# The decay exponents of a state-space layer: from TensorE products to rows read back from memory, GpSimd and ScalarE

## The chip, the cores and the metric

One core of one Trainium2 chip runs the whole program. The time is device microseconds of that core. TensorE (PE) multiplies and transposes, VectorE (DVE), ScalarE (ACT) and GpSimd (POOL) do the rest, and SyncE's queue (SP) starts nearly all transfers. The kernel before takes 5693.69 us, the median of 3 runs (5674.86 to 5695.94).

## The reference

Two transformer-like layers over 64 batches of 128 tokens with 256 channels, all in float32. Layer 0 is a state-space layer (Mamba-2 form), a cross attention and a mixture of 16 experts; layer 1 is an attention, a cross attention and a quantized product. Only the first matters here:

```python
dt = jax.nn.softplus(dt_in + dt_bias)          # 32 heads
A_bar = jnp.exp(-jnp.exp(A_log) * dt)
def step(h, inp):
    ab, dtt, bt, ct, xt = inp
    h = ab[..., None, None] * h + (dtt[..., None] * bt)[:, :, None, :] * xt[..., None]
    return h, jnp.einsum('bhn,bhpn->bhp', ct, h)
```

The kernel writes the recurrence as a product. With cum(t) the running sum of |A| dt up to token t, head h of token t gets the sum over s <= t of (C_t . B_s) exp(-(cum(t) - cum(s))) dt_s x_s. For each head this is a 128 x 128 matrix of exponents, 32 of them for a batch.

## The kernel before, in words

The program has three phases. The first takes each batch through four chains: M (norm, input projection, convolution, softplus), N (the exponents, the products of the heads, gate, output projection), X (cross attention of layer 0) and F (router, shared expert). They are pipelined over the batches: an iteration of the loop does M of batch n, N of n-1, X of n-2 and F of n-3. The second phase runs the experts, the third layer 1 in the same manner. The change touches only the first.

Each engine has its own instruction list, and the table ORDER (line 48) fixes by hand in which order it takes the steps of the four chains: `Nv3` is step v3 of chain N, `Mip1` step ip1 of chain M. Engines meet through semaphores: `tell` raises one, `done` waits for this batch's, `was` for the previous batch's. An engine never goes past a step that waits. `link` makes an engine wait for its own last result.

The way of the exponents before:

- DVE step Msp (lines 712 to 727): 18 small dependent operations on 128 x 32 tiles make softplus by a series, ending in `a`, the decay times dt, spread over the rows of `aGL`.
- PE step MGL: two products with the triangle `triu` make the running sums; ACT copies them to `GL`; POOL step MR (line 547) makes from them `R`, 128 x 1024, with a mask that picks a head in each row.
- PE steps Na0 to Na7 (line 1383): each multiplies 19 rows of GL by 19 rows of R, and so writes the differences of the running sums of four heads into a PSUM bank, 128 x 512.
- ACT Ne0 to Ne7 (line 1123) takes the exponential, DVE Nm0 to Nm7 (line 768) takes the minimum with 1 and multiplies with `cbm`, the masked C.B product, and PE Nv0 to Nv7 (line 1398) multiplies with x dt.

```python
tell(mm(Q[4 if k in (1, 3) else 2][:, :], GL[rows, 1, :], R[rows, 4 * u:4 * u + 4, :], start=True, stop=True), "arg")
tell(s_.activation(Edw[k % 2], Q[4 if k in (1, 3) else 2][:, :], ACT.Exp), "E")
tell(v.scalar_tensor_tensor(Mh[k % 2], Ed[k % 2], 1.0, cbm.unsqueeze(1).broadcast_to([P, 4, T]), ALU.min, ALU.mult), "M")
```

After the heads: ACT copies both banks (Yt), PE transposes them (Ny0, Ny1), DVE adds the skip term to `y2` (line 773) and multiplies with the gate `gz` (Nyg, line 778), ACT sums its squares (Nsq), POOL makes the root mean square (Nrms, lines 553 and 554), PE transposes (NyT) and projects (Npr), and DVE makes `x1` (Nx1, line 785). In the next iteration X norms x1: DVE statistics (Xln2, line 671), POOL (lines 539 and 540), DVE (Xln2n, line 675), PE transposition (Xln2n).

X scores its 16 heads in four strips of the key rows (line 1318, Xs0 to Xs3), each after a mask product (line 1417), in banks Q5, Q6, Q5, Q6. DVE takes row maxima (line 682), ACT exponentials (lines 1082 and 1085), PE transposes them (line 1324, Xt0 to Xt3), and DVE (line 693) and ACT (line 1092) evacuate two of the four each.

Of the kernel before, what the change touches and what calls it, by code (L numbers as in the profile page):

```python
# [13 lines left out]
F32 = mybir.dt.float32  # L14
# [6 lines left out]
ALU = mybir.AluOpType  # L21
# [3 lines left out]
P = 128  # L25
# [64 lines left out]
def two_layers(nc, x_d, ctx_d, m0_d, m1_d, w_in, conv_w, conv_b, a_log, d_p, dt_bias, norm_w, w_out,  # L90
# [5 lines left out]
    slot_d = nc.dram_tensor("slot_rows", (NB, T, 4), U32)  # L96
    with ExitStack() as ctx:
# [65 lines left out]
        Apos = sb("Apos", [P, NH])  # L163
# [11 lines left out]
        aGL = sb("aGL", [P, 2, P])  # L175
        pick = sb("pick", [P, 8])
# [8 lines left out]
        base = sb("base", [P, NE])  # L185
        table = sb("table", [1, 3, TILES], I32)
# [20 lines left out]
        cbm, GL, R = part(T), cut(part(2 * T), 2), part(8 * T).rearrange("p (h t) -> p h t", t=T)  # L207
        Edw, Mhw = [part(512), part(512)], [part(512), part(512)]
        Ed = [e.rearrange("p (h t) -> p h t", t=T) for e in Edw]
        Mh = [e.rearrange("p (h t) -> p h t", t=T) for e in Mhw]  # L210
        Yt = part(2 * DI)
        sq0, yT, yg, y2 = Edw[0], cut(Edw[1], IC), Mhw[0], Mhw[1]
# [52 lines left out]
        spread = lambda k: aGL[:, k, :].rearrange("p (i r) -> p i r", i=4)[:, :, 8 * k:8 * k + 8].rearrange("p i (u j) -> p u i j", u=2)  # L265

        for n in ("xa_in", "xr_in", "ctx0_in", "mask0_in", "meta_out", "xo_out", "meta_in", "x2s_in", "ctx1_in", "mask1_in", "out_done"):
            sig(n, 16)
        sig("scattered", 32)  # L270
        sig("gathered", 32)
        signals("M", "DVE", "ln1_var ln1_xn dt_pre a conv cbm xs2 gz xdt")
        signals("M", "PE", "ln1_Tps ip2 ip1 z CB GLps xsT")
        signals("M", "ACT", "ln1_T dt_abs bcT dt_exp xpad tz conv_th GL")
        signals("M", "POOL", "ln1_rstd R")
        signals("N", "DVE", "M:8 y2 yg x1")
        for n, k in (("arg", 8), ("Yk", 8), ("Yb", 2), ("yTps", 1), ("mamba", 1), ("E", 8), ("Yt", 2), ("ss", 1), ("yT", 1), ("rms", 1)):
            sig(n, k)
        signals("X", "DVE", "ln2_var ln2_xn mrow k0c S0max:4 PT0v:2 x2")
        signals("X", "PE", "ctxTps ln2_Tps k0 qv0 S0:4 PT0ps:4 PV0:2")  # L280
        signals("X", "ACT", "ctxT ln2_T q0c v0c P0:4 PT0s:2 OT0")
# [23 lines left out]
        links = {"M_DVE": 18, "X_DVE": 5, "F_DVE": 15, "A_DVE": 5, "K_DVE": 3, "L_DVE": 11, "M_POOL": 1, "N_POOL": 1, "X_POOL": 1,  # L305
# [65 lines left out]
        def _(sp):  # L371
# [126 lines left out]
        def _(pool):  # L498
# [1203 lines left out]
```

## Time and profile before

| | |
|---|---|
| median of 3 runs | 5693.69 us |
| the profiled execution's own time | 5707.57 us |
| its span | 5705.7 us |
| PE busy | 5197.1 us (91%) |
| DVE busy | 3886.4 us (68%) |
| ACT busy | 2510.9 us (44%) |
| POOL busy | 1489.5 us (26%) |
| mean granted TensorE clock | 0.876 |
| first phase | to about 2860 us |
| costliest line of the first phase | L1383, 684.7 us |

The profile of one execution lists for every engine what it was busy with, what it waited for, and which transfer or engine released it. Busy times of an engine can't be compared with the span alone: what counts is which of the waits ends last in the stage in question.
### The profile page before, as it was taken

The page shows a single profiled execution, that of the slowest core. Times are in us where ns is not written, and L with a number is a line of the kernel's source. Part 1 is how long each engine was busy: PE and PEld are TensorE (multiplying, and loading weights), DVE is VectorE, ACT ScalarE, POOL GpSimd, SP SyncE. Part 2 cuts the span into 40 slices and gives each one's busy share as a digit, 9 for nine tenths or more (in the row PEclk, how much of TensorE's full clock was granted, in tenths as well). Part 3 has the DMA queues.
Part 4 walks back from the last instruction along what each step waited for, and adds up shares of the span by engine and source line. Part 5 has one row for each costly group of instructions (what it writes and reads, how often), then busy time and mean ns, then how long its engine had stood idle before and what let it go on. Part 6 is the DMA issues. An engine that isn't in the chain of part 4 may idle for free.

```text
span 5705.7 us, 117447 instructions
## 1 busy us (share of the span) xinstructions
PE 5197.1 (91%) x33556; PEld 3331.3 (58%) x33683; DVE 3886.4 (68%) x10535; ACT 2510.9 (44%) x6582; POOL 1489.5 (26%) x2225
## 2 busy tenths in 40 slices
PE   5999999999999999999957779999999999999997
PEld 3656656656655665665535546666666666666564
DVE  3767776777776777776633337777777777777776
ACT  1444443444444444443322235555555555555554
POOL 1211121121121122112100014444444444344343
PEclk8878887888887888887767779999999999999999
DMA  3000000000000000000022210000000000000000
GB/s 103 19 17 17 17 22 17 18 20 17 17 22 17 17 20 18 17 17 22 16 74 88 88 45 19 18 18 18 18 18 18 18 18 18 18 18 18 14 18 13
DMA packets 153161, 146.76 MB, mean 26 GB/s; under 512 B 39392, under 2 KB 142112, under 8 KB 153120
## 3 DMA queue, kind: packets, MB, share of 16 engines
q1 hardware_dynamic: 134208, 102.98, 6.1%
q0 software_dynamic: 12288, 33.57, 1.9%
q10 hardware_dynamic: 6624, 9.70, 0.5%
q8 instruction: 21, 0.34, 0.0%
q14 instruction: 20, 0.16, 0.0%
HBM read 91.38 MB, written 54.79 MB: 26 GB/s over the span
## 4 chain that ended last, share of the span: by engine, by line
PE 49%; issue 20%; DVE 11%; POOL 9%; DMA 5%; ACT 3%; SPq 2%; POOLq 0%; DVEq 0%; ACTq 0%
PE Q L1288 11%; PE Q L1383 11%; PE Q L1295 6%; PE Q L1318 5%; PE Q L1300 4%; PE Q L1490 4%; PE Q L1398 4%; DMA arena<-in_ctx_dram 2%; POOL mvK L540 2%; POOL l L596 2%; DMA meta<-slot_rows 2%; DVE arena L739 2%; DVE arena L693 1%; PE Q L1502 1%; PE Q L1417 1%
## 5 line engine op out<-in xcount | busy, mean ns | idle before, releaser
L1300 PE MATMUL Q<-ident,arena 128*128 128x128 f32 x4768 | 847.5, 298 | 237.7 <-DVE arena L962 75.5
L1300 PEld LDWEIGHTS Q<-ident,arena 128*128 128x128 f32 x4768 | 589.6, 152 | 614.6 <-issue 244.7
L1383 PE MATMUL Q<-arena 19*128 19x512 f32 x1024 | 684.7, 828 | 47.3 <-ACT arena L1123 43.5
L1123 ACT ACTIVATE arena<-Q 128x512 f32<-128x512 f32 x512 | 300.0, 599 | 564.7 <-PE Q L1383 563.2
L1295 PE MATMUL Q<-Wkvl,arena 128*128 128x512 f32 x1024 | 513.2, 625 | 1.6 <-ACT arena L1074 0.9
L553 POOL TENSOR_TENSOR ss<-ss,eps 128x1 f32<-128x1 f32 x64 | 12.2, 191 | 1918.2 <-ACT arena L1133 1918.2
L596 POOL TENSOR_TENSOR l<-l,half_pow 128x8 f32<-128x8 f32 x192 | 330.0, 1719 | 583.5 <-DVE l L958 583.5
L682 DVE TENSOR_REDUCE mx<-Q 128x4 f32<-128x512 f32 x512 | 351.0, 686 | 54.6 <-PE Q L1318 33.1
L768 DVE SCALAR_TENSOR_TENSOR arena<-arena 128x512 f32<-128x512 f32 x512 | 348.8, 687 | 50.0 <-ACT arena L1123 49.1
L1318 PE MATMUL Q<-arena 32*128 32x128 f32 x4096 | 374.0, 284 | 9.1
L1318 PEld LDWEIGHTS Q<-arena 32*128 32x128 f32 x4096 | 312.6, 187 | 116.5 <-issue 116.5
L1324 PEld LDWEIGHTS Q<-ident,arena 128*128 128x128 f32 x2048 | 245.3, 142 | 111.1 <-issue 68.5
L1262 ACT ACTIVATE arena<-Q,mxl 128x256 f32<-128x256 f32 x512 | 236.6, 474 | 158.4 <-DVE mxl L994 158.4
L1085 ACT ACTIVATE arena<-Q,mx 128x128 f32<-128x128 f32 x1024 | 291.1, 375 | 1.4 <-DVE mx L682 1.4
L1324 PE MATMUL Q<-ident,arena 128*128 128x128 f32 x2048 | 289.1, 274 | 1.2 <-ACT arena L1082 0.5
L1383 PEld LDWEIGHTS Q<-arena 19*128 19x128 f32 x1024 | 168.6, 227 | 203.0 <-issue 103.0
L1295 PEld LDWEIGHTS Q<-Wkvl,arena 128*128 128x128 f32 x1024 | 186.6, 201 | 170.6 <-issue 155.0
L1490 PE MATMUL Q<-Wgu,arena 128*128 x576 | 212.2, 503 | 72.4 <-issue 54.6
L1071 ACT ACTIVATE arena<-Q 128x256 f32<-128x256 f32 x256 | 98.3, 384 | 388.3 <-PE Q L1300 388.3
L1288 PE MATMUL Q<-arena,Win 128*128 128x128 f32 x1536 | 252.3, 314 | 0.0
L1288 PEld LDWEIGHTS Q<-arena,Win 128*128 128x128 f32 x1536 | 215.7, 217 | 62.0 <-issue 62.0
L1398 PE MATMUL Q<-arena 128*16 128x128 f32 x4096 | 243.5, 330 | 0.0
(292 smaller groups left out, 10672.7 us busy)
## 6 DMA issues: line engine op xcount, KB each, us to landing
arena<-routed_rows SPq DMA_DIRECT2D x144, 128.0 KB, 2.0
expert_rows<-arena SPq DMA_DIRECT2D x144, 128.0 KB, 1.7
arena<-in_x_dram SPq DMA_DIRECT2D x128, 128.0 KB, 2.1
arena<-in_ctx_dram SPq DMA_DIRECT2D x128, 128.0 KB, 2.2
x_rows<-arena SPq DMA_DIRECT2D x64, 128.0 KB
arena<-x_rows SPq DMA_DIRECT2D x64, 128.0 KB, 2.0
out_dram<-arena SPq DMA_DIRECT2D x64, 128.0 KB, 1.7
routed_rows<-arena SPq DMA_DIRECT2D x17, 128.0 KB, 1.7
```

The lines of the kernel that those rows point to most:

```text
L596: link(pool, "K_POOL", b, g.tensor_tensor(l2[:, k, :], l2[:, k, :], half_pow[:, :], ALU.pow), bare=True)
L682: largest = v.tensor_reduce(mx[:, 4 * j:4 * j + 4], pj, AX.X, ALU.max, negate=True)
L768: tell(v.scalar_tensor_tensor(Mh[k % 2], Ed[k % 2], 1.0, cbm.unsqueeze(1).broadcast_to([P, 4, T]), ALU.min, ALU.mult), "M")
L1123: tell(s_.activation(Edw[k % 2], Q[4 if k in (1, 3) else 2][:, :], ACT.Exp), "E")
L1288: last = mm(out, lhs(c), rhs(c), start=c == 0, stop=c == n - 1)
L1295: last = mm(out, lhs(c), rhs(c), start=c == 0, stop=c == n - 1)
L1300: last = nc.tensor.transpose(out[:, c * P:(c + 1) * P], src[:, c * P:(c + 1) * P], ident[:, :])
L1318: last = mm(banks[j][:, g * T:(g + 1) * T], QT[r, g, :], KT[r, g // 2, :], start=False, stop=g == NG - 1)
L1324: last = nc.tensor.transpose(bank[:, g * T:(g + 1) * T], S[:, j, g, :], ident[:, :])
L1383: tell(mm(Q[4 if k in (1, 3) else 2][:, :], GL[rows, 1, :], R[rows, 4 * u:4 * u + 4, :], start=True, stop=True), "arg")
L1398: last = mm(Q[3 + k // 4][32 * i:32 * i + HP, (k % 4) * T:(k % 4 + 1) * T], xdt[:, h * HP:(h + 1) * HP], Mh[k % 2][:, i, :], start=True, s ...
L1490: last = mm(Q[2 + s % 2][:, 0:2 * FF], xeT[s % 4][:, c, :], Wgu[:, bass.ds(e, 1), c, :].rearrange("p a f -> p (a f)"), start=c == 0, stop= ...
```

## The change

The exponents no longer come from TensorE. The running sums go out to a table in memory (`cum_rows`), 32 x 128 floats for a batch, and come back in four loads, each of which gives all 128 partitions the same 1024 values (8 heads x 128 tokens) in one of four tiles `Ew`. POOL subtracts from each the partition's own sum (Nd0 to Nd3), ACT takes the absolute value and then exp(-x) in place (Ng, Ne), and the product with `cbm` follows in place, for three tiles on DVE (Nm0 to Nm2), for the fourth on POOL (Nm3). PE takes eight heads in one step (Nv0 to Nv3). The tiles `R`, `GL`, `aGL` and `pick` go, with what sets them up.

Further: the softplus series moves from DVE to POOL, in another form (terms in pairs, 13 operations behind `ratio`); the gate product Nyg moves from DVE to POOL; cross attention has a third PSUM bank, Q2, so that strips 0, 1 and 2 are scored in one step; and ACT makes all four of its evacuations. ORDER is rewritten for all five queues.

```diff
@@ ORDER[1]
         "SP": """
-            Xc Nx Mx Fm Fo
+            Ncb0 Xc Ncb1 Ncb2 Ncb3 Nx Mx Fm Mco Fo
         "POOL": """
-            Xx1r Fln3 Xln2 Mln1 Nrms Fsc MR
+            Xx1r Xln2 Fln3 Nd0 Mln1 Nd1 Nd2 Nd3 Nm3 Msp Fsc Nyg Nrms
...
@@ SP
+                yield "co"
+                done(sp, "cumT", b)
+                tell(sp.dma_start(rows(cum_d, b), cumT[0:NH, :]), "cum_out", 16)
...
+                for j in range(4):
+                    yield f"cb{j}"
+                    if j == 0:
+                        done(sp, "cum_out", b, 16)
+                    was(sp, "Yk", b, j + 1)
+                    heads8 = cum_d[bass.ds(b, 1), 8 * j:8 * j + 8, :].rearrange("a h t -> (a h t)")
+                    tell(sp.dma_start(Ew[j], heads8.partition_broadcast(P)), f"wide{j}", 16)
@@ POOL
+                yield "sp"
+                J = lambda ins: link(pool, "M_POOL", b, ins, bare=True)
+                s, z, z2, z4 = dts[:, 2, :], dts[:, 3, :], dts[:, 4, :], dts[:, 5, :]
+                done(pool, "ratio", b)
+                J(g.tensor_tensor(z, s, s, ALU.mult))
+                tell(g.tensor_tensor(z2, z, z, ALU.mult), "square")
+                J(g.tensor_tensor(terms, coef[:, 0, :, :], z.unsqueeze(1).broadcast_to([P, 4, NH]), ALU.mult))
...
+                J(g.tensor_tensor(dts[:, 6, :], terms[:, 0, :], dts[:, 0, :], ALU.add))
+                tell(g.tensor_tensor(dts[:, 7, :], dts[:, 6, :], Aneg[:, :], ALU.mult), "a")
...
+                    yield f"d{j}"
+                    if j == 0:
+                        done(pool, "cums", b)
+                    done(pool, f"wide{j}", b, 16)
+                    tell(g.tensor_tensor(E8[j], E8[j], cums[:, 8 * j:8 * j + 8].unsqueeze(2).broadcast_to([P, 8, T]), ALU.subtract), "diff")
+                yield "m3"
+                done(pool, "E", b, 4)
+                done(pool, "cbm", b)
+                tell(g.tensor_tensor(E8[3], E8[3], cbm.unsqueeze(1).broadcast_to([P, 8, T]), ALU.mult), "M3")
+                yield "yg"
+                done(pool, "y2", b)
+                tell(g.tensor_tensor(yg, gz, y2, ALU.mult), "yg")
@@ DVE
                 J(v.tensor_scalar(dts[:, 5, :], u, 2.0, None, ALU.add))
                 J(v.reciprocal(dts[:, 5, :], dts[:, 5, :]))
-                J(v.tensor_tensor(s, u, dts[:, 5, :], ALU.mult))
...
+                tell(v.tensor_tensor(dts[:, 2, :], u, dts[:, 5, :], ALU.mult), "ratio")
...
-                for k in range(8):
-                    yield f"m{k}"
...
+                for j in range(3):
+                    yield f"m{j}"
+                    done(dve, "E", b, j + 1)
+                    tell(v.tensor_tensor(E8[j], E8[j], cbm.unsqueeze(1).broadcast_to([P, 8, T]), ALU.mult), "M")
@@ ACT
+                tell(s_.activation(cums, Q[0][:, 2 * T:2 * T + NH], ACT.Copy), "cums")
+                tell(s_.activation(cumT[0:NH, :], Q[0][0:NH, 3 * T:4 * T], ACT.Copy), "cumT")
...
+                for j in range(4):
+                    yield f"g{j}"
+                    done(act, "diff", b, j + 1)
+                    tell(s_.activation(Ew[j], Ew[j], ACT.Abs), "gap")
+                    yield f"e{j}"
+                    done(act, "gap", b, j + 1)
+                    tell(s_.activation(Ew[j], Ew[j], ACT.Exp, scale=-1.0), "E")
@@ PE
-                for k in range(2):
-                    last = mm(Q[0][:, (2 + k) * T:(3 + k) * T], aGL[:, k, :], triu[:, :], start=True, stop=True)
...
+                mm(Q[0][:, 2 * T:2 * T + NH], triu[:, :], dts[:, 7, :], start=True, stop=True)
+                tell(mm(Q[0][0:NH, 3 * T:4 * T], dts[:, 7, :], triu[:, :], start=True, stop=True), "cumps")
...
-                strips(b, banks, (0, 1), QT0, KT0, 0, mask)
-                for j in (2, 3):
-                    yield f"s{j}"
-                    done(pe, "S0max", b, j - 1)
-                    strips(b, banks, (j,), QT0, KT0, 0, mask)
+                strips(b, banks, (0, 1, 2), QT0, KT0, 0, mask)
+                yield "s3"
+                done(pe, "S0max", b)
+                strips(b, banks, (3,), QT0, KT0, 0, mask)
```

TensorE at the head of the loop's body, before: line 1300 transposes the context, line 1383 are the exponent products, line 1398 the heads, and the third row of line 1300 is the transposition of the normed x1.

```order
L1300 MATMUL Q<-ident,arena 128x128 x2
L1383 MATMUL Q<-arena 128x512 x2
L1383 MATMUL Q<-arena 128x512
L1398 MATMUL Q<-arena 16x128 x4
L1383 MATMUL Q<-arena 128x512
L1398 MATMUL Q<-arena 16x128 x4
L1300 MATMUL Q<-ident,arena 128x128 x2
L1383 MATMUL Q<-arena 128x512
L1288 MATMUL Q<-Wr,arena 128x16 x2
L1300 MATMUL Q<-ident,arena 128x128 x2
```

And now (the lines are those of the changed file; 1311 transposes, 1299 multiplies, 1395 are the heads):

```order
L1311 MATMUL Q<-ident,arena 128x128 x2
L1311 MATMUL Q<-ident,arena 128x128 x2
L1299 MATMUL Q<-arena,Wk 128x128 x4
L1311 MATMUL Q<-ident,arena 128x128 x2
L1299 MATMUL Q<-arena,Wq 128x128 x4
L1299 MATMUL Q<-Wr,arena 128x16 x2
L1311 MATMUL Q<-ident,arena 128x128 x2
L1299 MATMUL Q<-Wv,arena 128x256 x2
L1299 MATMUL Q<-Win,arena 128x32 x2
L1299 MATMUL Q<-arena,Win 128x128 x4
L1395 MATMUL Q<-arena 16x128 x8
```

The transposition of the normed x1 has moved from behind the fourth exponent product and two heads' steps to the second place, and the first heads' step stands behind the input projection's first piece.

GpSimd in one body of the loop now, from the last subtractions to the root mean square (576 are the subtractions, 580 the product m3, 552 to 568 the series, 604 the scatters of F, 583 the gate product):

```order
L576 TENSOR_TENSOR arena<-arena 128x1024 x3
L580 TENSOR_TENSOR arena<-arena 128x1024
L552 TENSOR_TENSOR arena<-arena 128x32
L553 TENSOR_TENSOR arena<-arena 128x32
L554 TENSOR_TENSOR arena<-coef,arena 128x128
...
L568 TENSOR_TENSOR arena<-arena,Aneg 128x32
L604 DMA routed_rows<-arena,meta 133248x256 x2
L583 TENSOR_TENSOR arena<-arena 128x512
L586 TENSOR_TENSOR ss<-ss,eps 128x1
L587 TENSOR_TENSOR ss<-ss,half_pow 128x1
```

Before, this queue had only the small steps of the norms, the scatters and one 1024-wide product in a body; series and gate product were VectorE's. Now both scatters stand between the series and the gate product.

## Rows read from the trace of the kernel before

**Rows 1.** Windows of the whole program: length, busy of PE, PEld, DVE, ACT, POOL, granted clock, DMA

```profile
1000.00:2300.00 1300.00, 1258.34 (x8313) 784.48 (x8312) 938.28 (x2873) 553.49 (x1394) 257.54 (x360) 0.82 0.06 18
...
2850.00:2950.00 100.00, 52.42 (x203) 34.26 (x203) 35.64 (x91) 17.16 (x55) 2.76 (x4) 0.62 0.22 67
```

**Rows 2.** Line 547, one instruction in an iteration: number, duration, first and last start

```profile
L547 POOL TENSOR_TENSOR arena<-arena,pick x64: 1895/1908/2132, 70.7 to 2792.0; 128x1024 f32<-128x1024 f32 x64
```

**Rows 3.** Windows of single iterations of the first phase, same columns, last the sum and mean of 16

```profile
1400.73:1441.44 40.71, 39.29 (x276) 24.88 (x275) 30.94 (x96) 18.27 (x46) 8.73 (x13) 0.87 0.06 19
1441.44:1488.24 46.80, 45.38 (x275) 27.90 (x274) 30.86 (x95) 18.27 (x46) 8.72 (x12) 0.74 0.05 17
...
sum 685.94, PE 663.50 PEld 414.46 DVE 495.65 ACT 292.29 POOL 137.02; mean PE 41.47 PEld 25.90 DVE 30.98 ACT 18.27 POOL 8.56
```

**Rows 4.** Windows of 2 us, PE busy, granted clock, DMA share and GB/s

```profile
1542.00:1544.00 2.00, 2.00 (x3) 0.50 0.00 0
...
1574.00:1576.00 2.00, 2.00 (x12) 1.00 0.69 223
```

**Rows 5.** Groups by line, window 1000 to 2300, the operations that go

```profile
L1383 PE MATMUL Q<-arena 19*128 19x512 f32 x482 | 319.0, 818 | 20.4 <-ACT arena L1123 20.4
...
L768 DVE SCALAR_TENSOR_TENSOR arena<-arena 128x512 f32<-128x512 f32 x243 | 165.3, 687 | 16.0 <-ACT arena L1123 15.7
L1123 ACT ACTIVATE arena<-Q 128x512 f32<-128x512 f32 x242 | 141.9, 599 | 261.6 <-PE Q L1383 261.6
...
L547 POOL TENSOR_TENSOR arena<-arena,pick 128x1024 f32<-128x1024 f32 x30 | 57.3, 1909 | 0.6
...
L693 DVE COPY arena<-Q 128x512 f32<-128x512 f32 x60 | 40.9, 682 | 0.0
...
L721 DVE SCALAR_TENSOR_TENSOR arena<-arena 128x32 f32<-128x32 f32 x180 | 34.5, 192 | 6.1
```

**Rows 6.** Timeline of PE, window 1536 to 1579

```profile
1538.24 1.12 PE L1383 MATMUL Q<-arena 19*128 19x512 f32 x2 [0.68 <-ACT arena L1123]
...
1560.78 1.15 PE L1318 MATMUL Q<-arena 32*128 32x128 f32 x8
```

**Rows 7.** Timeline of PE in the third phase

```profile
4432.16 1.17 PE L1318 MATMUL Q<-arena 32*128 32x128 f32 x24
```

**Rows 8.** Groups by line, window 1000 to 2300, rows that bound the new operations

```profile
L571 POOL DMA_INDIRECT routed_rows<-arena,meta x60 | 60.8, 1014 | 17.6 <-issue 17.6
...
L1082 ACT ACTIVATE arena<-arena 128x512 f32<-128x512 f32 x62 | 35.3, 620 | 0.0
...
L560 POOL TENSOR_TENSOR arena<-arena,bv0b 128x256 f32<-128x256 f32 x30 | 21.7, 724 | 37.4 <-DVE arena L805 37.4
...
L539 POOL TENSOR_TENSOR mvX<-mvX,eps 128x1 f32<-128x1 f32 x30 | 17.7, 588 | 12.9 <-DVE mvX L672 12.8
...
L553 POOL TENSOR_TENSOR ss<-ss,eps 128x1 f32<-128x1 f32 x30 | 5.7, 191 | 895.5 <-ACT arena L1133 895.5
```

**Rows 9.** Timeline of all engines, window 1539 to 1541.5

```profile
1538.83 0.42 DVE L671 BATCH_NORM_STATS2 stX<-arena 128x6 f32<-128x256 f32 x1
...
1539.51 0.69 DVE L768 SCALAR_TENSOR_TENSOR arena<-arena 128x512 f32<-128x512 f32 x1
...
1539.66 0.59 POOL L539 TENSOR_TENSOR mvX<-mvX,eps 128x1 f32<-128x1 f32 x1 [0.99 <-DVE mvX L672]
...
1540.97 0.41 DVE L675 TENSOR_SCALAR arena<-arena,mvX 128x256 f32<-128x256 f32 x1 [0.44 <-POOL mvX L540]
```

**Rows 10.** Windows of DVE alone, from the convolution of one iteration to its end

```profile
1562.50:1577.02 14.52, 12.53 (x34) 1.00 0.11 36
```

**Rows 11.** Windows of 2 us in the third phase, same columns

```profile
4412.00:4414.00 2.00, 0.48 (x3) 1.00 0.23 67
...
4416.00:4418.00 2.00, 2.00 (x4) 0.50 0.23 66
...
4420.00:4422.00 2.00, 2.00 (x12) 1.00 0.00 0
```

More of the change, by code:

```diff
@@ L206, in two_layers @@
         bcT, dts = cut(part(2 * T), 2), cut(part(8 * NH), 8)
[L207 to L210, printed above, removed]
+        terms = cut(part(4 * NH), 4)
+        cbm, cumT, cums = part(T), part(T), part(NH)
+        Ew = [part(8 * T) for _ in range(4)]
+        E8 = [e.rearrange("p (h t) -> p h t", t=T) for e in Ew]
         Yt = part(2 * DI)
-        sq0, yT, yg, y2 = Edw[0], cut(Edw[1], IC), Mhw[0], Mhw[1]
+        sq0, yT = Yt[:, 0:DI], cut(Yt[:, DI:2 * DI], IC)
+        yg, y2 = part(DI), part(DI)
         xr, x1, x1r, x2, o0 = part(D), part(D), part(D), part(D), part(D)
@@ L512, in _ @@
             g.memset(triu[:], 1.0)
-            g.memset(aGL[:], 0.0)
-            g.memset(pick[:], 0.0)
             g.memset(before[:], 1.0)
+            for k in range(8):
+                g.memset(coef[:, 1 - k % 2, k // 2, :], 2.0 / (2 * k + 1))
             g.memset(ones[:], 1.0).then_inc(SEM["pads"], 1)
@@ L525, in _ @@
                             pattern=[[1, P]], channel_multiplier=-1)
-            picked = [(32 * i + 8 * k, -1) for i in range(4) for k in range(2)] + [(32 * i + 16 + c, 0) for i in range(4) for c in range(3)]
-            for n, (row, step) in enumerate(picked):
-                g.affine_select(out=pick[:, :], in_=pick[:, :], compare_op=ALU.not_equal, fill=1.0, base=-row,
-                                pattern=[[step, 8]], channel_multiplier=1).then_inc(SEM["pads"], 1)
-                pool.wait_ge(SEM["pads"], n + 2)
             g.affine_select(out=causal[:, :, :], in_=causal[:, :, :], compare_op=ALU.is_ge, fill=NEG, base=0,
@@ L631, in _ @@
             dve.wait_ge(SEM["consts"], 1)
-            rows = aGL[:, :, :].rearrange("p k (i r) -> p k i r", i=4)
-            for k in range(2):
-                v.memset(rows[0:1, k, :, 8 - 8 * k:16 - 8 * k], 1.0)
-            for c in range(3):
-                here, after = slice(32 * c, 32 * c + 1), slice(32 * c + 32, 32 * c + 33)
-                v.memset(rows[here, 0, :, 16 + c:17 + c], 1.0)
-                v.memset(rows[after, 0, :, 16 + c:17 + c], -1.0)
-                v.memset(rows[after, 1, :, 16 + c:17 + c], BLOCKED)
             for bank in (Q[3], Q[4]):
@@ L745, in M @@
                 done(dve, "CB", b)
-                was(dve, "M", b, 8)
+                was(dve, "M3", b)
                 tell(v.tensor_tensor(cbm, Q[0][:, 0:T], triu[:, :], ALU.mult), "cbm")
@@ L756, in M @@
                 done(dve, "xsT", b)
-                was(dve, "Yk", b, 8)
+                done(dve, "a", b)
+                was(dve, "Yk", b, 4)
                 was(dve, "y2", b)
@@ L787, in X @@
             def X(b):
-                banks = (Q[5], Q[6], Q[5], Q[6])
+                banks = (Q[6], Q[2], Q[5], Q[6])
                 yield "ln2"
@@ L1086, in softmax, with evac @@
                     tell(last, f"P{n}")
-            def evac(b, banks, PT, n):
-                for j in (1, 3):
+            def evac(b, banks, PT, n, js=(1, 3)):
+                for j in js:
                     yield f"t{j}"
@@ L1154, in X @@
                 yield from softmax(b, banks, S0, mx0, 0)
-                yield from evac(b, banks, PT0, 0)
+                yield from evac(b, (Q[2], Q[5], Q[6], Q[2]), PT0, 0, range(4))
                 yield "OT"
@@ L1339, in M @@
                 yield "ln1n"
-                was(pe, "GL", b)
+                was(pe, "cumT", b)
                 lnT("ln1", xn0, Q[0], b)
@@ L1413, in X @@
             def X(b):
-                banks = (Q[5], Q[6], Q[5], Q[6])
+                banks = (Q[6], Q[2], Q[5], Q[6])
                 def mask(bank):
```

164 lines of the change are left out of this document (65 added, 99 removed).

## The prediction

> **What bounds the kernel now.** I read the windows first. In the steady part of the first phase TensorE is busy 97% of the time, VectorE 72%, ScalarE 43% and GpSimd 20% [rows 1]. One R product of GpSimd comes in each iteration, 64 of them from 70.7 to 2792.0 us, so an iteration takes 2721.3/63 = 43.2 us [rows 2]. TensorE works 41.5 us of it [rows 3]. The kernel's first half is bound by TensorE, and 1 us less in an iteration is worth 64 us. The third phase and the expert phase are not touched.
>
> The clock belongs to this reading. Iterations take 40.7 us at a granted clock of 0.87 and 46.8 us at 0.74 [rows 3]. The clock is at one of two levels, 1.2 or 2.4 GHz, so the low time is 2 x (1 - 0.87) x 40.7 = 10.6 us in the one and 24.3 us in the other. 6.1 us more for 13.7 us of low time: a low microsecond costs 0.44 us. The mean clock of 0.82 [rows 1] means 15.6 us of low time, 6.9 us an iteration. It falls soon after the iteration's head, where two short waits and the 19-row exponent products lie, and stays low with TensorE fully busy [rows 4].
>
> **TensorE.** The eight exponent products go: 319.0 us in 1300 us, 10.5 us an iteration [rows 5]. At the full clock one is 1.12 us [rows 6]. Cross attention's scores of strips 0, 1 and 2 are now one step over three banks. Before, strip 2 was a step of its own, 1.15 us [rows 6]; in the third phase, which has this form, three strips take 1.17 us together [rows 7]. That is 1.1 us less. The two cumulative products get smaller, 0.3 us. So 41.5 - 10.5 - 1.1 - 0.3 = 29.6 us of work stay, at the present mix of clocks.
>
> **The other engines**, in an iteration. VectorE loses eight 512-wide products (5.45 us), 13 of the 32-wide steps (2.5 us), two 512-wide evacuations (1.36 us) [rows 5] and one 512-wide gate product (0.7 us). It gains three 1024-wide ones; 512 take 0.687 us and 32 take 0.192, so 1024 take 1.21 us, 3.6 us. 31.0 becomes 24.6 us. ScalarE: eight 512-wide exponentials (4.8 us) go, eight 1024-wide passes come. A 512-wide one between SBUF tiles is 0.620 us [rows 8]; twice is 1.24, and with some 0.2 us of start-up counted once it is 1.04, 8.3 us in all. With two evacuations of 0.6 us more, 18.3 becomes 23.1 us. GpSimd: the one 1.91 us product becomes five of that size (9.5 us), a 512-wide one (between 0.72 us for 256 and 1.91 us for 1024: 1.1 us) and 13 small dependent steps. Nothing shows such a step on GpSimd. Its bounds are 0.19 us (one element) and 0.72 us (256 elements) [rows 8], plus 0.07 us to the next: 3.4 to 10.3 us for 13. Most have 32 elements, two have 128; I take 0.42 us each, 5.5 us. 8.6 becomes about 22 us. So no engine's work alone reaches TensorE's 29.6 us. What the order makes them wait for decides.
>
> **The new chain.** The iteration ends with x1, and its first dense step is the transposition of the normed x1, second in TensorE's new order. Before, three exponent products and more stood ahead of it. From the statistics to the normed rows took 2.55 us, 1538.83 to 1541.38 [rows 9]. The statistics can start 0.7 us after TensorE's last product, and the 0.4 us transposition of the context covers little. TensorE is idle for about 3 us at each head, against 43.2 - 41.5 = 1.7 us in a whole iteration before.
>
> The second piece is longer. The softplus series starts from `ratio`, which VectorE now makes after the last row maximum of cross attention. In the window from the convolution to the iteration's end VectorE is busy 12.5 us [rows 10]; less a maximum, the two evacuations and the gate product, and with the last sum, 10.2 us stay behind `ratio`. So 24.6 - 10.2 = 14.4 us of work stand ahead of it, and waits: for both norms' GpSimd answers, the second of them behind the first 1.91 us subtraction, for the first exponential (1.9 + 2 x 1.04 us after its data), for the rank product, for the scores. I estimate 7.6 us, and `ratio` at 22 us after x1. Then, in GpSimd's order, the series (5.5), the two scatters (1.01 each and 0.3 between [rows 8], 2.6 us) and the gate product (1.1), then on TensorE the transpositions NyT, MxsT and XOT and the projection (about 0.9, 0.9, 0.9, 1.9 us), then x1 (0.7 with its wait), and 0.2 us of handovers. 22 + 5.5 + 2.6 + 1.1 + 4.6 + 0.7 + 0.2 = 36.7 us. This is over TensorE's 29.6 + 3 = 32.6 us, so my forecast is that TensorE waits, mainly ahead of NyT: **36.7 us an iteration**. 43.2 - 36.7 = 6.5 us, times 64 is 416 us. The profiled execution's own time is 5707.6 us, 14 us above the median of the runs shown; 5707.6 - 416 = 5292, rounded **5290 us**.
>
> **SP and DMA.** An iteration adds 16 KB out and four loads of 512 KB. A window with a DMA share of 0.69 moved 223 GB/s [rows 4], so 2 MB need 6.5 us at the full 323 GB/s. The first waits for the sums, about 5 us before x1; the context load stands behind it, the x load behind all four. I place x at 3.0 us after x1, just when VectorE wants it: hidden, with no slack. The set-up loses 0.6 us of VectorE's and about 6 us of GpSimd's selections; those lie under the weight loads.
>
> **A rule against the change.** VectorE's 512-wide product of two SBUF tiles ran from 1539.51 to 1540.20; GpSimd's one-element sum, started at 1539.66, took 0.59 us [rows 9], against 0.191 us for the same sum elsewhere [rows 8]. It ended when the product did. So the two block each other. The Trainium skill (SBUF — State Buffer, Who interferes with whom) says the same: an instruction of VectorE with two SBUF inputs and one of GpSimd that reads SBUF exclude each other for the whole instruction. The trace agrees. I have 1.5 us of such waits in the 7.6.
>
> For the long subtractions I took the 1.91 us of the R product [rows 2], the same engine, width and kind. The Trainium skill (GPSIMD Engine Reference, Elementwise — side-by-side cycle accounting) gives 4497 ns for a sum of 2048 elements; an estimate from that page is 2.25 us for 1024, by which the five would take 1.7 us more and the iteration would be up to 38.4 us. The row decides.
>
> **Rivals.**
> **1. TensorE stays the bound.** If `ratio` and the series come earlier than I estimate, the head alone counts: 29.6 + 3.2 = 32.8 us, 10.4 x 64 = 666 us, 5040 us. For it: my 7.6 us are a guess. Against it: gate product and scatters stand in line behind the series.
> **2. The loads are late.** At half the rate the 2 MB take 6.5 us longer; x, last in line, arrives some 4.5 us late, and VectorE's list slips with it: 41.2 us, 5580 us. Against it: the window's 223 GB/s.
> **3. The two engines lock.** The three 1024-wide VectorE products each wait for most of a 1.91 us subtraction, and half the series' steps take the 0.59 us of [rows 8] or more: some 3.5 + 1 us, again 41 us, 5580 us. Against it: before the change one iteration shows only a few such meetings, but it has only one long GpSimd product.
> **4. The clock stays low: slower.** The 29.6 us hold about 3.7 us of low-clock cost that remains (6.9 less the removed products' own share of 3.2: 10.5 us as they ran, 7.3 at the full clock, where one pair runs side by side and another beside the scores): 25.9 us at the full clock. If TensorE, waiting more often, is granted 2.4 GHz for a fraction 1 - f of the time, the iteration is 25.9 + 3 + 0.44 f P. It passes the old 43.2 at f = 0.75 (clock 0.62). At f = 0.8 it is 44.6 us, plus 90 us, 5798 us; at f = 1, 51.6 us. For it: a stretch with TensorE busy 52% has a clock of 0.62 [rows 1]. Against it: in the third phase an idle head of 1.5 us in 2 costs one low stretch, and dense products bring the clock back within 6 us [rows 11]; behind the new head come dense 128-row products, not the 19-row ones.
>
> **Chances and range.** Forecast 0.46 (its own range 35 to 39 us: 5180 to 5440), rival 1 0.22, rival 2 0.09, rival 3 0.10, rival 4 0.09, no change 0.04 (gains and waits just cancel). A measurement of this kernel tells 0.5% (28 us) from nothing. Faster: 0.46 + 0.22 + 0.09 + 0.10 = 0.87; same 0.04; slower 0.09. From 5000 to 5600 us only rival 4, the null case and the edges are left out, 2 in 10; the bounds of the series (2.1 us less or 4.8 more, times 64: 5155 to 5600) lie inside.
>
> **What the new profile should show.** No 19-row products; PE busy near 30 us in an iteration of 36 to 38; idle TensorE at the head for the normed x1 (3 us) and ahead of NyT for GpSimd's product (over 1 us); `ratio` at 22 us; series steps of 0.3 to 0.5 us; the 1024-wide subtraction near 1.9 us; a clock of 0.8 to 0.9. Wrong would be: the wide loads as the releaser of GpSimd or of the first statistics (rival 2), subtractions or steps far over these sizes (rival 3), a clock under 0.65 (rival 4), or a period under 34 us (rival 1).

## The result and the profile after

The changed kernel takes 5699.2 us (median of 20 runs, 5691.2 to 5713.7) and the kernel before 5683.6 us (20 runs). The ratio is 1.0028, with a 95% interval of 1.0018 to 1.0037: no difference worth the name, where 5290 us had been forecast. The profiled execution has a span of 5694.8 us. The windows after, with the columns of [rows 1] and [rows 3]; the second line is one iteration of the first phase, from the end of one x1 nearly to the end of the next:

```profile
1000.00:2300.00 1300.00, 980.45 (x7676) 736.59 (x7675) 968.40 (x2209) 681.62 (x1458) 679.93 (x896) 0.84 0.20 67
...
1578.57:1622.40 43.83, 31.99 (x258) 24.17 (x258) 32.10 (x75) 22.77 (x49) 22.78 (x30) 0.84 0.21 70
```

x1 comes 37 times from 926.6 to 2492.5 us, so an iteration takes 43.5 us, as against 43.2 before. What TensorE does has fallen, from 1258 to 980 us in this stretch, or 41.5 to 32.0 us an iteration (29.6 had been forecast), at nearly the same clock (0.82, then 0.84). All of it came back as idle time: TensorE now stands still for 12 us of 44. VectorE was to fall from 31.0 to 24.6 us and is still at 32.1. The waits of the same stretch (what waited for what: us in total, times, longest):

```profile
PE Q L1311 <- DVE arena L699: 145.5, 66, 5.3
DVE arena L768 <- POOL arena L583: 109.4, 30, 3.7
...
DVE stM L695 <- DMA arena<-in_x_dram: 74.0, 30, 3.6
...
PE Q L1311 <- POOL arena L583: 63.4, 30, 2.1
PE Q L1311 <- DMA arena<-in_ctx_dram: 54.6, 30, 3.2
PE Q L1376 <- POOL arena L568: 38.2, 30, 1.4
```

L699 is VectorE's normalization ahead of the transpositions, L583 GpSimd's gate product, L695 the statistics of the next batch's x, L568 the end of the softplus series. Three different things hold TensorE: slow norms, late loads, and the gate product. The next groups by line (shapes apart; busy, mean ns of one, idle before) say why the norms are slow:

```profile
L576 POOL TENSOR_TENSOR arena<-arena 128x1024 f32<-128x1024 f32 x120 | 255.8, 2152 | 0.0
L781 DVE TENSOR_TENSOR arena<-arena 128x1024 f32<-128x1024 f32 x90 | 148.1, 1645 | 0.0
L580 POOL TENSOR_TENSOR arena<-arena 128x1024 f32<-128x1024 f32 x30 | 87.4, 2913 | 240.9 <-ACT arena L1135 240.9
L699 DVE TENSOR_SCALAR arena<-arena,mvF 128x256 f32<-128x256 f32 x30 | 59.3, 1976 | 3.6
L699 DVE TENSOR_SCALAR arena<-arena,mvM 128x256 f32<-128x256 f32 x30 | 59.3, 1975 | 28.1 <-POOL mvM L543 28.1
L829 DVE TENSOR_SCALAR rt<-rt 128x16 f32<-128x16 f32 x30 | 50.3, 1677 | 1.1
L739 DVE TENSOR_SCALAR arena<-arena 128x32 f32<-128x32 f32 x29 | 33.3, 1148 | 0.0
...
L699 DVE TENSOR_SCALAR arena<-arena,mvX 128x256 f32<-128x256 f32 x30 | 12.4, 412 | 4.0
```

The same 256-wide normalization takes 412 ns for mvX and 1976 ns for mvF and mvM; a step of 16 columns takes 1677 ns. The timeline of an ordinary iteration (start, us, engine, line; VectorE, GpSimd and TensorE rows) shows what runs beside them:

```profile
1580.32 0.41 DVE L699 TENSOR_SCALAR arena<-arena,mvX 128x256 f32<-128x256 f32 x1
1580.58 0.66 PE L1311 MATMUL Q<-ident,arena 128*128 128x128 f32 x4 [3.17 <-DMA arena<-in_ctx_dram]
1581.11 1.89 POOL L576 TENSOR_TENSOR arena<-arena 128x1024 f32<-128x1024 f32 x1
1581.18 1.98 DVE L699 TENSOR_SCALAR arena<-arena,mvF 128x256 f32<-128x256 f32 x1
...
1586.22 0.43 DVE L695 BATCH_NORM_STATS2 stM<-arena 128x6 f32<-128x256 f32 x1 [3.07 <-DMA arena<-in_x_dram]
...
1587.85 6.63 POOL L576 TENSOR_TENSOR arena<-arena 128x1024 f32<-128x1024 f32 x3
1587.92 1.98 DVE L699 TENSOR_SCALAR arena<-arena,mvM 128x256 f32<-128x256 f32 x1 [0.94 <-POOL mvM L543]
1589.95 0.69 PE L1311 MATMUL Q<-ident,arena 128*128 128x128 f32 x2 [5.05 <-DVE arena L699]
1590.23 2.50 DVE L781 TENSOR_TENSOR arena<-arena 128x1024 f32<-128x1024 f32 x1
1592.83 1.68 DVE L829 TENSOR_SCALAR rt<-rt 128x16 f32<-128x16 f32 x1
...
1606.00 0.19 DVE L741 TENSOR_TENSOR arena<-arena 128x32 f32<-128x32 f32 x1
```

Each norm starts just after a subtraction (L576) and ends just after it: 1581.18 + 1.98 is 1583.16, the subtraction ended at 1583.00. It doesn't run slowly, it stands until GpSimd is done. That looks like the lock of [rows 9], on instructions that had not been counted. The three subtractions in a row (6.63 us, where three times 1.89 would be 5.67) hold the third norm, then the first product, then the router step, which ends at 1594.51, when the last of them has ended (1594.48). The 1.0 us beyond 5.67 is about what the last subtraction would have to wait for the end of the product (1592.73): VectorE seems to hold GpSimd in turn. The end of the same iteration:

```profile
1612.35 0.25 POOL L568 TENSOR_TENSOR arena<-arena,Aneg 128x32 f32<-128x32 f32 x1 [0.18 <-POOL arena L567]
...
1612.73 0.40 PE L1376 MATMUL Q<-arena,triu 128*128 128x32 f32 x2 [1.40 <-POOL arena L568]
...
1613.21 1.28 POOL L604 DMA_INDIRECT routed_rows<-arena,meta  x1 [0.61 <-issue]
...
1615.79 1.27 POOL L583 TENSOR_TENSOR arena<-arena 128x512 f32<-128x512 f32 x1
1617.11 2.82 PE L1311 MATMUL Q<-ident,arena 128*128 128x128 f32 x12 [2.11 <-POOL arena L583]
1617.17 0.69 DVE L768 SCALAR_TENSOR_TENSOR arena<-arena,Q 128x512 f32<-128x512 f32 x1 [3.65 <-POOL arena L583]
1617.78 0.42 DVE L855 TENSOR_TENSOR arena<-Q,arena 128x256 f32<-128x256 f32 x1
...
1622.28 0.48 DVE L795 SCALAR_TENSOR_TENSOR arena<-Q,ss,arena 128x256 f32<-128x256 f32 x1 [0.33 <-PE Q L1306]
```

GpSimd's gate product (L583) stands behind the series and two scatters. VectorE's gate for the next batch (L768) must not write `gz` before that product has read it, so VectorE waits 3.65 us. Behind it stands `xo` (L855), and for `xo` waits a store that is ahead of all loads in SP's queue. SP's own timeline, around the end of the iteration before:

```profile
1570.85 0.35 SPq L412 DMA_DIRECT2D cum_rows<-arena  x1
1575.03 0.34 SPq L439 DMA_DIRECT2D x_rows<-arena  x1
1576.08 0.35 SPq L421 DMA_DIRECT2D arena<-cum_rows  x1
1576.71 0.35 SPq L429 DMA_DIRECT2D arena<-in_ctx_dram  x1
1577.35 0.25 SPq L431 DMA_DIRECT2D mask0i<-in_mask_BxS_ik_dram  x1
1577.97 1.44 SPq L421 DMA_DIRECT2D arena<-cum_rows  x3
1579.66 0.33 SPq L424 DMA_DIRECT2D arena<-in_x_dram  x1
1580.27 0.33 SPq L409 DMA_DIRECT2D arena<-in_x_dram  x1
```

The first wide load goes out at 1576.08, 2.5 us before the end of x1 (1578.57); the two loads of x are last, behind 2 MB. From 1578 to 1584, in windows of 1 us, the share of the DMA engines is 0.92 to 1.10 and they move 239 to 384 GB/s: the loads are not slow, they are asked for late.

TensorE's clock, in windows of 2 us of the same iteration (length, PE busy, granted clock, DMA share, GB/s):

```profile
1586.00:1588.00 2.00, 0.00 (x0) 0.56 0.00 0
1590.00:1592.00 2.00, 2.00 (x6) 0.50 0.00 0
1598.00:1600.00 2.00, 2.00 (x27) 1.00 0.04 1
```

It falls to its lower level while TensorE stands still for 5.05 us, and stays there for some 7.5 us of dense products behind the wait. Around the wait of 2.11 us at the end it falls again (0.50 from 1618 to 1620); behind the 3.17 us at the head it was 1.00.

### The profile page after: what moved, and what is told of

Same layout as the page of the kernel before. It is cut to its first block, busy times and chain, and to the rows that moved or that the text cites. A ratio compares the mean times of both kernels' runs of the same rounds, so it can differ in the third digit from the quotient of the medians.

```text
span 5694.8 us, 115799 instructions
## 1 busy us (share of the span) xinstructions
PE 4605.1 (81%) x32658; PEld 3218.1 (57%) x32659; DVE 3970.2 (70%) x9179; ACT 2805.1 (49%) x6774; POOL 2398.2 (42%) x3363
## 4 chain that ended last, share of the span: by engine, by line
issue 32%; POOL 23%; PE 20%; DVE 14%; ACT 5%; DMA 2%; SPq 2%; POOLq 1%; DVEq 1%; ACTq 0%
PE Q L1306 7%; PE Q L1311 4%; PE Q L1486 4%; POOL arena L580 3%; POOL mvK L543 2%; POOL arena L576 2%; POOL l L629 2%; ACT arena L1132 2%; DMA meta<-slot_rows 2%; DVE rt L829 2%; PE Q L1299 2%; POOL arena L583 1%; POOL routed_rows L604 1%; PE Q L1329 1%; PE Q L1498 1%
## 5 line engine op out<-in xcount | busy, mean ns | idle before, releaser
L1311 PE MATMUL Q<-ident,arena 128*128 128x128 f32 x4768 | 861.1, 306 | 764.6 <-DVE arena L699 346.4
L576 POOL TENSOR_TENSOR arena<-arena 128x1024 f32<-128x1024 f32 x256 | 545.6, 2152 | 7.8 <-DMA arena<-cum_rows 7.8
L580 POOL TENSOR_TENSOR arena<-arena 128x1024 f32<-128x1024 f32 x64 | 186.1, 2908 | 510.7 <-ACT arena L1135 510.7
L781 DVE TENSOR_TENSOR arena<-arena 128x1024 f32<-128x1024 f32 x192 | 315.4, 1643 | 3.4 <-ACT arena L1135 3.4
L1329 PEld LDWEIGHTS Q<-arena 32*128 32x128 f32 x4096 | 251.4, 188 | 102.7 <-issue 102.7
L1335 PE MATMUL Q<-ident,arena 128*128 128x128 f32 x2048 | 307.0, 279 | 0.5 <-ACT arena L1091 0.5
L1329 PE MATMUL Q<-arena 32*128 32x128 f32 x4096 | 300.6, 285 | 0.0
L1132 ACT ACTIVATE arena<-arena 128x1024 f32<-128x1024 f32 x256 | 269.3, 1052 | 7.9 <-POOL arena L576 7.9
L1135 ACT ACTIVATE arena<-arena 128x1024 f32<-128x1024 f32 x256 | 269.5, 1053 | 6.1
L1299 PEld LDWEIGHTS Q<-arena,Win 128*128 128x128 f32 x1536 | 243.1, 237 | 46.8 <-issue 46.7
L1299 PE MATMUL Q<-arena,Win 128*128 128x128 f32 x1536 | 267.1, 329 | 0.0
L1101 ACT ACTIVATE arena<-Q 128x512 f32<-128x512 f32 x384 | 232.7, 614 | 54.2 <-PE Q L1335 54.2
```

The costliest lines, as they stand in the source:

```text
L576: tell(g.tensor_tensor(E8[j], E8[j], cums[:, 8 * j:8 * j + 8].unsqueeze(2).broadcast_to([P, 8, T]), ALU.subtract), "diff")
L580: tell(g.tensor_tensor(E8[3], E8[3], cbm.unsqueeze(1).broadcast_to([P, 8, T]), ALU.mult), "M3")
L781: tell(v.tensor_tensor(E8[j], E8[j], cbm.unsqueeze(1).broadcast_to([P, 8, T]), ALU.mult), "M")
L1132: tell(s_.activation(Ew[j], Ew[j], ACT.Abs), "gap")
L1299: last = mm(out, lhs(c), rhs(c), start=c == 0, stop=c == n - 1)
L1311: last = nc.tensor.transpose(out[:, c * P:(c + 1) * P], src[:, c * P:(c + 1) * P], ident[:, :])
```

## The experiments

Ratios are to the kernel before, timed beside each, with 95% intervals; the changed kernel's is 1.0028, and what a repair gives is counted from there, in times of 5684 us.

**The locks.** The subtraction on one column only:

```diff
-  tell(g.tensor_tensor(E8[j], E8[j], cums[:, 8 * j:8 * j + 8].unsqueeze(2).broadcast_to([P, 8, T]), ALU.subtract), "diff")
+  tell(g.tensor_tensor(Ew[j][:, 0:1], Ew[j][:, 0:1], cums[:, 8 * j:8 * j + 1], ALU.subtract), "diff")
```

> Leaves out the subtraction of the running sums but for one column of each wide tile, so the exponents are not the reference's; everything that waits for it still does. Theory L (the long GpSimd instructions block VectorE's: the norms of F and M, the first exponent product and the router's scaling took 1.98, 1.98, 2.50 and 1.68 us instead of 0.41, 0.41, 1.21 and 0.23, some 5.9 us in an iteration of 43.3): these go back to their short times, VectorE's ratio comes 4 to 5 us earlier after x1 (26 us now), the iteration falls to about 38.5 us, the total to about 5390. Theory D (the loads come too late: the x rows at 6.2 us after x1, the context at the head): the wait for the x rows only grows by what the norm of F gains, ratio comes at most 2.5 us earlier, total 5530 or more.

Measured: 5539.3 us, 0.9733 (0.9715 to 0.9751), in the range of Theory D and not at the 5390 of Theory L. The norms are back at 413 ns, the products at 1219, the router step at 234: the locks were real. But the wait for x grows from 74.0 us in 30 iterations to 146.9 in 32, because the statistics are now ready for it earlier:

```profile
DVE stM L695 <- DMA arena<-in_x_dram: 146.9, 32, 5.7
...
PE Q L1311 <- DVE arena L699: 119.1, 41, 5.4
DVE arena L768 <- POOL arena L583: 113.2, 31, 3.7
```

So the subtractions cost 168 us even while the load is late, and the load's wait takes up part of what they free. This is not the price of the locks alone, since GpSimd's queue has also become shorter.

**Which instructions lock.** The same, and fills of about the subtraction's length behind it, which read nothing:

```diff
+  g.memset(dump[:, j, :], 0.5)
+  tell(g.memset(Ew[j][:, 1:], 0.5), "diff")
```

> Leaves out the same subtraction, but GpSimd is kept as long as before at each of the four places, some 1.9 us, by two fills that read nothing. Told apart: if what counts is only that GpSimd's reads meet VectorE's second input, VectorE's norms and products run at their short times and the total is within 1% of that with one column. If fills block as well (every long GpSimd instruction locks), the norms of F and M (one SBUF input) stay near 2 us and the total near 5690. Theory D expects near 5690 too, but with short norms and a longer wait for the x rows.

Measured: 5651.4 us, 0.9923 (0.9906 to 0.9940), between the two totals named: 112 us above the run with one column, 60 under the changed kernel. Groups of VectorE by line:

```profile
L784 DVE TENSOR_TENSOR arena<-arena 128x1024 f32<-128x1024 f32 x90 | 109.5, 1217 | 0.0
...
L702 DVE TENSOR_SCALAR arena<-arena,mvF 128x256 f32<-128x256 f32 x31 | 55.5, 1789 | 3.7
L702 DVE TENSOR_SCALAR arena<-arena,mvM 128x256 f32<-128x256 f32 x31 | 55.3, 1784 | 28.9 <-POOL mvM L544 28.9
```

The product of two tiles runs free beside a fill (1217 ns, 1645 on average beside subtractions, which hold one in three); the norm, with one tile as input, is still held (1789 ns), and so is the router step (1518 ns). There are two kinds of lock, and the second needs no read on GpSimd's side. With the products free and the norms held, most of what the one-column run had gained is gone again.

**The loads.** SP issues the loads of x ahead of the wide ones:

```diff
-  Ncb0 Xc Ncb1 Ncb2 Ncb3 Nx Mx Fm Mco Fo
+  Xc Mx Ncb0 Ncb1 Ncb2 Ncb3 Nx Fm Mco Fo
```

> SP's order is Xc Mx Ncb0 Ncb1 Ncb2 Ncb3 Nx Fm Mco Fo: context and x rows are asked for ahead of the four wide loads. Theory D: VectorE's wait for the x rows (1.6 us at 1541 us, up to 3.6) and most of TensorE's wait for the context (54.6 us in 30 iterations, 1.8 each) go; 2 to 3.5 us an iteration, total 5470 to 5570. Theory L: M's statistics come earlier but its norm then waits for the GpSimd answer behind the next subtraction, or the wide loads come later; under 1 us an iteration, total 5640 or more.

Measured: 5546.6 us, 0.9737 (0.9720 to 0.9755), as Theory D had it. The wait for x is gone from the list. In the iteration of this kernel that begins with x1's end at 1530.96, the statistics of x start at 1535.47, 4.5 us later instead of 7.65 (1578.57 to 1586.22 above). The order also changes the locks: the first wide load comes later, and the norm of F takes 1158 ns on average instead of 1976, since some of them no longer meet a subtraction.

**The gate product**, back on VectorE behind y2:

```diff
@@ POOL
-  Msp Fsc Nyg Nrms
+  Msp Fsc Nrms
@@ DVE
-  Ny0 Ny1 Mxs2
+  Ny0 Ny1 Nyg Mxs2
```

> The gate product goes back from GpSimd to VectorE, right behind the skip sums; nothing else. Theory Q (the gate product stands behind series and scatters in GpSimd's queue; TensorE waits 2.1 us for it ahead of the projection, VectorE 3.65 us with the gate of the next batch, and behind that the residual, its store and the context load): both waits go, the iteration falls 2.5 to 4 us, total 5440 to 5540. Rival: VectorE is what bounds, and 0.7 us more of work costs 45 us: 5740.

Measured: 5535.3 us, 0.9723 (0.9707 to 0.9740), in the range of Theory Q. Both waits are gone. Left are TensorE's for the norms (143.7 us) and the loads: 95.7 us of TensorE's for the context and 106.9 us of VectorE's for x, in 32 iterations.

**The series**, back on VectorE in its old form, the rest as changed:

> The series from `ratio` to the decay steps goes back to VectorE in its old form; the rest stays as changed. On GpSimd it takes 6.3 us from `ratio`, on VectorE (from the 0.22 us between its instructions before) about 2.9. Theory P (the slow series is part of the bound, TensorE's 1.3 us ahead of the cumulated steps being its cost): 5694 - 64 x 1.3 = about 5610. Theory Q (what binds is the wait of the gate product's tail and the late loads; the convolution now starts 2.9 us later instead, and the cumulated steps wait for it): 5640 to 5740, no gain. I expect Q.

Measured: 5744.1 us, 1.0094 (1.0066 to 1.0121), slower than the changed kernel itself and 4 us above the range of Q. So moving GpSimd's 6.4 us series back gains nothing: VectorE has the work instead, and what follows on it comes later (VectorE busy 1013.83 of 1300 us, where it was 968.40).

**Both repairs**, loads and gate:

> The two correct repairs together: the loads of the residual and of the next input ahead of the wide loads, and the gate product back on VectorE. Alone they gave 0.9737 and 0.9723. If each removes a wait of its own (additive), the product is 0.947, about 5390. If both only free the same start of the next iteration (the late loads hide behind the gate's tail), they give little more than one alone: 5480 to 5540. I expect the first, 5370 to 5430, with TensorE's wait for the second and third norm (VectorE held by the wide subtraction) as the largest that is left.

Measured: 5341.7 us, 0.9386 (0.9363 to 0.9408), 28 us under the range expected. Alone they gave 165 and 173 us, together 365, somewhat more than the sum of 339; the excess is little more than the error of the four ratios. One reason for it shows: the norm of F is at 458 ns, so that together the two repairs also take away nearly all of that lock. As expected, what is left is the norm, now that of M (1976 ns):

```profile
PE Q L1311 <- DVE arena L696: 171.0, 71, 4.0
```

Not all of this is lock. VectorE waits 98.1 us in 35 iterations for the GpSimd steps of that norm, which stand behind the first subtraction in GpSimd's queue.

**Both repairs and the one-column subtraction:**

> As the run with both repairs, and the wide subtraction over one column only, so that GpSimd does none of the 1024-wide subtractions (this leaves the subtraction out of all but one column). What this gains over the run with both repairs is the price of the two engines holding each other when nothing else covers it. Theory L (6.8 us of lock waits per iteration lie ahead of `ratio`, 2 to 5 of them on the path): 130 to 300 us under that run, 5100 to 5270. Theory T (TensorE, at 32 us of work per iteration, binds before that): not under 5200.

Measured: 5091.9 us, 0.8954 (0.8922 to 0.8985), just under the range of Theory L. With the other two causes away, the subtractions cost 250 us, 3.9 us an iteration. VectorE's wait for the GpSimd steps of M's norm falls from 2.8 to 1.2 us an iteration, so part of the price is place in a queue and part is locks; the two were not told apart further. The profiled span is 5088.9 us, and x1 comes every 33.8 us (40 from 909.9 to 2226.4): close to the 32.8 us of rival 1.

**Without wide work on GpSimd**: the subtraction goes into ScalarE's absolute value, the fourth product and the gate product are VectorE's, the loads of x first:

```diff
@@ ACT
-  tell(s_.activation(Ew[j], Ew[j], ACT.Abs), "gap")
+  for i in range(8):
+      last = s_.activation(E8[j][:, i, :], E8[j][:, i, :], ACT.Abs, bias=cums[:, 8 * j + i:8 * j + i + 1])
+  tell(last, "gap")
@@ POOL
-  Xx1r Xln2 Fln3 Nd0 Mln1 Nd1 Nd2 Nd3 Nm3 Msp Fsc Nyg Nrms
+  Xx1r Xln2 Fln3 Mln1 Msp Fsc Nrms
```

(`cums` is copied with its sign turned.)

> A version meant to beat both: no 1024-wide work on GpSimd at all. ScalarE subtracts inside its absolute value (8 of 128 columns per tile with a bias per head, about 0.29 us each, 2.3 us per tile instead of 1.05), the fourth product goes to VectorE (1.2 us), the gate product too, and the two loads go first; the series stays on GpSimd. ScalarE has then 27.5 us of work per iteration, VectorE about 26. If the locks were what was left, it comes near the run without the subtraction: 5150 to 5300. If ScalarE's chain (13 us for the four tiles, in order with the softmax) becomes the wait, 5350 to 5450. I expect 5230.

Measured: 5205.3 us, 0.9151 (0.9128 to 0.9173): the whole computation, 8.5% faster than the kernel before. Its window and its largest waits of TensorE:

```profile
1000.00:2300.00 1300.00, 1069.89 (x9451) 791.64 (x9445) 1010.74 (x2773) 1009.15 (x2819) 419.12 (x879) 0.95 0.24 81
```

```profile
PE Q L1305 <- DVE arena L686: 83.0, 36, 3.3
...
PE Q L1329 <- ACT arena L1081: 63.2, 36, 1.8
```

An iteration is 35.6 us (x1 41 times from 916.1 to 2339.1). TensorE's clock is 0.95, and its work 29.3 us an iteration, where it was 32.8 on average at 0.84: a part of what the repairs give comes back through the clock. No run tells that part apart.

**The fourth product alone**, taken from GpSimd in the kernel with both repairs:

> As the run with both repairs (5342 us, 0.9386), and the fourth product moved from GpSimd (2.91 us there, 1.22 us on VectorE), so that of the wide work only the subtractions stay on GpSimd. Theory L (GpSimd's and VectorE's wide work hold each other): the 1.0 us by which the first small instruction of the ratio is held goes, but VectorE has 1.2 us more: 5310 to 5370, no clear change; the gain of the version without wide work on GpSimd then comes from the subtractions. Theory M (the fourth product alone was the trouble): near that version's 5205.

Measured: 5343.2 us, 0.9396 (0.9370 to 0.9422), the same as the kernel with both repairs (0.9386). What the version without wide work gains over that kernel, 138 us, is therefore the doing of where the subtractions are made, since that is all that still differs. It is a net gain: ScalarE's work rises by it.

**Two variants of that version.** The series back on VectorE:

> As the version with ScalarE's subtraction (5205 us, 0.9151), and the series back on VectorE. There TensorE waits for GpSimd's series once in 36 iterations, so nothing is to be gained ahead of the cumulated steps, and VectorE, busy 27.6 of 36.1 us, gets 2.9 us more ahead of the convolution: 5210 to 5290. If the series on GpSimd was a cost, it would fall under 5190.

Measured: 5318.5 us, 0.9353 (0.9327 to 0.9379), 113 us slower and above my range. TensorE, which had waited for the series once in 36 iterations, now waits for VectorE's series and for its products. And two places of the order changed:

```diff
@@ DVE
-  Fr Nm0 Ftop
+  Fr Ftop Nm0
@@ ACT
-  Ng0 Ne0 Mln1n
+  Ng0 Mln1n Ne0
```

> As the version with ScalarE's subtraction (5205 us), with two places of the order changed: VectorE does the router ahead of the first product (the router waits 2.3 us behind a product that waits for ScalarE), and ScalarE evacuates the first norm's transposes between the first tile's absolute values and its exponential (TensorE waits 1.0 us on average there). If these waits are on the path: 64 x 1 to 2 us, 5080 to 5150. If they are only moved to the first product: 5180 to 5210.

Measured: 5367.7 us, 0.9429 (0.9399 to 0.9460): 162 us slower, against both of my expectations. The waits say where:

```profile
PE Q L1386 <- DVE arena L768: 127.0, 34, 3.8
...
DVE rt L833 <- PE Q L1453: 96.6, 34, 3.1
```

The first tile's product is now late for TensorE's first exponent step, and behind that step in TensorE's queue stands the rank product for which VectorE waits in turn. The 2.3 us that the router had waited were cheaper than what replaced them. Which of the two changes did it was not told apart; TensorE's clock is 0.90 in this kernel, not 0.95. Not tried: the loads of x in another engine's queue, which would tell the place in the queue from the sharing of the DMA engines.

## Why the prediction was wrong

The step that failed is "`ratio` at 22 us after x1": the term of lock waits in it (1.5 us) was far too small, and the load of x was put at nothing.

**TensorE's work.** 29.6 us of work were forecast. In the changed kernel it is 32.0 us in the iteration shown and 32.8 on average (980.45 of 1300 us, times 43.5), at a clock of 0.84; with all three causes away it is 29.2 us (1036.28 us from 1000 to 2200) at 0.92, and the iteration 33.8. So the work came out at 29.6 only once the waits were gone and the clock was higher. That the exponent products and the third bank's step would pay was right; the 10 us were there to be had.

**The work of the others.** ScalarE 23.1 forecast, 22.8 measured. GpSimd about 22 forecast (the terms add up to 22.8), 22.8 measured, but by luck: subtractions and fourth product took longer than 1.91 us, the steps of the series less than 0.42. VectorE 24.6 forecast, 32.1. Its own work was right (the product 1219 ns once nothing locks it, 1.21 forecast); the rest is standing in locks.

**The chain, term by term**, in the iteration from 1578.57 to x1's end at 1622.76, 44.2 us:

- `ratio` at 22 us: it ends at 1606.19, 27.6 us after x1. This is the failed step, 5.6 of the 7.5 us by which the sum was too small. Of the 27.6 us VectorE is busy 21.55, of which 6.8 are locks and 14.7 its own work (14.4 forecast).
- the series 5.5 us: 6.4. Steps of 0.24 to 0.52 us with 0.18 us between where I had 0.07.
- the scatters 2.6: 3.2, half of the excess by a gap of 0.61 us ahead of the first.
- the gate product 1.1: 1.27. From it to x1 5.5: 5.7.

**The two parts of the failed step.** First the locks: "I have 1.5 us of such waits in the 7.6." They are 1.57 (second norm) + 1.57 (third) + 1.28 (first product) + 1.44 (router step) + 0.96 (first step of `ratio`) = 6.8 us, each its time here less its time alone; the first of them lies under the wait for x. I had taken the rule from a product of two tiles [rows 9] and looked for partners of that kind; four of the five are instructions with one tile as input.

Second the loads: "I place x at 3.0 us after x1, just when VectorE wants it: hidden, with no slack." VectorE wanted it 4.6 us after x1 and got it at 7.65, a wait of 3.07 us. Of the 4.65 us by which x was later than placed, 2.5 are the start: I had the first wide load 5 us before x1, and it came 2.5 us before, since SP's queue stood at the store of `xo`. The other 2.1 us are the stretch from there to x, 10.1 us where I had 8.0: SP needs until 1580.27 to issue them all, and context and two loads of x come on top of the 2 MB. The rate was not short of mine (up to 384 GB/s, 323 assumed).

The other 6.1 of the 7.6 us (7.6 less 1.5) were for waits on other engines. VectorE's idle time before `ratio` is 6.07 us, which looks right and is luck: half of it is the wait for x, and the waits for the exponential, the rank product and the scores, which I had in mind, hardly came.

**What was not in the sum at all.** The gate product on GpSimd was costed on the path to x1, but not for who must wait until it has read `gz`: VectorE 3.65 us, `xo`, the store, the next loads, TensorE's first transposition (3.17 us). Its repair alone gave 173 us, as much as either of the others (168 and 165). It also takes the product itself from behind the scatters, for which TensorE waited 2.11 us, and no run tells the two apart.

**The rivals.** Rivals 2 and 3 name what happened, and neither had its mechanism. Rival 2 had the loads late by a halved rate: its sign came (a load releases the first statistics of x), but the rate was full, and the loads were asked for late. Rival 3 had every 1024-wide product held and half the steps of the series slow: one product in three was held, the steps took 0.24 to 0.52 us, and the locks fell on the norms and the router. Their prices added, 4.5 us each on 36.7, make 45.7 us, and measured were 43.5; with other mechanisms behind it, that is near by chance. "No change" was described, with 0.04, as gains and waits that cancel: that is what happened. Rival 1 (5040 us) is nearly what came without the three causes (5092 us, with most of the subtraction left out). Rival 4's slower kernel did not come, the clock being 0.84 on average. But something of its mechanism is in the trace: behind two of TensorE's three long waits the clock is at its lower level, and in the fastest complete version, where the waits are shorter (3.3 us at most in the rows shown), it is 0.95.

**The rule.** What I cited was half of it. The Trainium skill (SBUF — State Buffer, Who interferes with whom) has also that an instruction of VectorE in a two-port mode contends with GpSimd, without the condition that GpSimd reads, and counts `tensor_scalar`, the form of the norm and the router step, among those that can enter such a mode. The fill beside the norm agrees (1789 ns against 413), and so does the product that a fill leaves alone. The estimate of 2.25 us for a subtraction can be judged too: free of locks it took 1.89 us, the R product's time. The fourth product, of the same width, took 2.35 us at its shortest.

## What to carry to other kernels

Before wide work goes to GpSimd, list every VectorE instruction that will run beside it, the short one-input ones too, and price each at the whole of GpSimd's instruction. For each operation that moves to another engine, follow not only who waits for its output, but who waits until it has read its inputs, and what stands behind those in the queues, SP's too. When rivals are mechanisms that can happen together, add their prices: here three causes took back all of a 10 us gain, and removing one gave about a quarter of what removing all three gave. And a wait of TensorE can cost more than its length: behind the one of 5.05 us here it ran at half the clock for some 7.5 us.

## What the runs showed of the hardware

A fill on GpSimd, which reads nothing, holds VectorE's one-input 256-wide instruction (1789 ns against 413), but not its product of two tiles (1217 ns). A 16-column step takes 1677 ns beside subtractions and 234 alone. GpSimd's product L580, the size of a 1.89 us subtraction, takes 2913 ns; it began at 1602.63, 0.7 us before the end of VectorE's product of 1602.10. In the run with both repairs and the one-column subtraction its median is 2375 ns and its shortest 2351, so about 0.54 us of the 2913 is that meeting and the rest its own length. Loads that give 512 KB to the 128 partitions take 5.6 us from issue to landing (median); a 128 KB load of x behind four of them took 6.2 us, and 2.1 us before the change:

```profile
arena<-cum_rows SPq DMA_DIRECT2D x120, 512.0 KB, 5.6
arena<-in_x_dram SPq DMA_DIRECT2D x60, 128.0 KB, 6.2
```
